# Sending each token to its chosen expert alone, in a fused attention and mixture-of-experts kernel

## What is computed

```python
logits = xt @ Wg.T
top1 = jnp.argmax(logits, axis=-1)
xhat = (xt - mu) * rsqrt(var + LN_EPS)
for e in range(8):                       # 256 -> 64 -> 256 each
    h = gelu((xhat * s_e + b_e) @ w1_e + bb1_e)      # exact gelu
    y += (top1 == e)[:, None] * (h @ w2_e + bb2_e)
```

## Time and profile before

| | us |
|---|---|
| median of 3 runs | 345.05 (344.06 to 345.36) |
| the profiled execution | 345.35 |
| its span, first to last instruction | 343.6 |
| PE busy | 318.1 (93%) |
| DVE busy | 234.1 (68%) |
| POOL busy | 146.3 (43%) |
| ACT busy | 138.3 (40%) |
| DMA queue 1 | 14.94 MB, 12.9% of 16 engines |

### The profile page before, as it was taken

The page is one execution under the profiler, slowest core; times in us unless marked ns, Lnnn a source line. Parts: engine busy times, 40 slices in busy tenths (PEclk is TensorE's granted clock), DMA queues, the critical chain, the costliest instruction groups (busy, mean ns, idle before and its releaser), DMA issues.

```text
span 343.6 us, 7930 instructions
## 1 busy us (share of the span) xinstructions
PE 318.1 (93%) x3240; PEld 271.2 (79%) x3256; DVE 234.1 (68%) x528; ACT 138.3 (40%) x209; POOL 146.3 (43%) x190
## 2 busy tenths in 40 slices
PE   2499889999899999999899998999899999998995
PEld 2388678797788977798787977889787988777794
DVE  6798794658758495675947587584947677573554
ACT  2356644504363243622455053632436234632310
POOL 4454724840548105760258305580048500470443
PEclk9999999999999999999999999999999999999999
DMA  7300400005000130005000050002200030001201
GB/s 264 138 1 2 124 0 4 2 2 183 3 2 2 60 125 0 2 2 169 17 2 3 0 185 2 2 1 84 103 1 2 2 122 2 3 2 61 63 2 61
DMA packets 13907, 15.49 MB, mean 45 GB/s; under 512 B 672, under 2 KB 12976, under 8 KB 13872
## 3 DMA queue, kind: packets, MB, share of 16 engines
q1 hardware_dynamic: 13696, 14.94, 12.9%
q10 hardware_dynamic: 176, 0.05, 0.1%
HBM read 10.80 MB, written 4.19 MB: 44 GB/s over the span
## 4 chain that ended last, share of the span: by engine, by line
PE 71%; DVE 16%; issue 4%; ACT 4%; POOL 2%; DVEq 0%; POOLq 0%; ACTq 0%
PE ring L182 17%; PE ring L184 16%; PE ring L183 15%; DVE energy L680 5%; PE ring L268 5%; PE ring L263 4%; DVE e_neg L671 3%; DVE stats L643 2%; PE ring L191 2%; PE ring L197 2%; PE ring L216 2%; PE kv_bank L237 2%; DVE qT L674 1%; PE ring L305 1%; PE ring L251 1%
## 5 line engine op out<-in xcount | busy, mean ns | idle before, releaser
L966 POOL TENSOR_TENSOR h_lo<-h,h_hi 128x512 fp32r<-128x512 f32 x32 | 41.1, 1287 | 23.5 <-DVE h_hi L710 23.0
L923 POOL TENSOR_SCALAR eps_var<-mv 128x4 f32<-128x4 f32 x8 | 1.9, 236 | 101.6 <-DVE mv L649 101.6
L182 PE MATMUL ring<-xn_hi,w_hi 128*128 128x512 f32 x96 | 41.1, 428 | 2.4 <-DVE xn_lo L661 1.5
L680 DVE TENSOR_TENSOR energy<-ring,causal 128x512 f32<-128x512 f32 x64 | 39.5, 679 | 0.0
L184 PE MATMUL ring<-xn_hi,w_lo 128*128 128x512 f32 x96 | 38.6, 402 | 0.0
L183 PE MATMUL ring<-xn_lo,w_hi 128*128 128x512 f32 x96 | 38.6, 402 | 0.0
L183 PE MATMUL ring<-w_lo,h_hi 128*128 128x256 f32 x128 | 35.8, 280 | 0.0
L184 PE MATMUL ring<-w_hi,h_lo 128*128 128x256 f32 x128 | 35.8, 280 | 0.0
L182 PE MATMUL ring<-w_hi,h_hi 128*128 128x256 f32 x128 | 35.8, 280 | 0.0
L540 ACT ACTIVATE e_neg<-ring,cols 128x512 f32<-128x512 f32 x32 | 22.0, 690 | 34.1 <-PE ring L184 29.7
L563 ACT ACTIVATE h<-ring,h_bias 128x512 f32<-128x512 f32 x32 | 22.3, 696 | 31.5 <-remote 13.1
(11 more groups left out here) (130 smaller groups left out, 846.0 us busy)
## 6 DMA issues: line engine op xcount, KB each, us to landing
x_in<-in_x SPq DMA_DIRECT2D x8, 512.0 KB, 4.4
o<-in_x SPq DMA_DIRECT2D x8, 512.0 KB, 3.6
out<-o SPq DMA_DIRECT2D x7, 512.0 KB, 3.1
energy<-in_w_in SPq DMA_DIRECT2D x4, 256.0 KB, 4.8
energy<-in_w SPq DMA_DIRECT2D x2, 512.0 KB, 6.9
out<-o SPq DMA_DIRECT2D x2, 256.0 KB, 2.1
sq<-in_w_o SPq DMA_DIRECT2D x1, 256.0 KB, 7.4
cols<-in_cols ACTq DMA_DIRECT2D x1, 32.0 KB
```

Source lines behind the costliest of these rows:

```text
L182: pe.matmul(bk, w_h(k), x_h(k), start=(first and k == 0), stop=False, skip_group_check=skip)
L680: dve.tensor_tensor(energy[:, t, m, :].rearrange("p (c n) -> p c n", c=CH), bank(f"s{t}{m}", n)[:, :].rearrange("p (c x) -> p c x", c=CH), ...
L966: pool.tensor_tensor(h_lo[:, m, :], h[m % 2][:, :], f32(h_hi[:, m, :]), ALU.subtract).then_inc(s["h_lo"], 1)
```

## The change

The dense expert computation is taken out of the ticks. In its place:

- **Counting and booking.** PE multiplies the one-hot choices with a triangular matrix and one of ones (`count_choices`, bf16, 8 small matmuls), DVE copies the 40 counts out, and POOL works out for each token its row in a list of blocks of 128 rows, each block of one expert (`book`: 24 instructions on 8 to 32 elements a partition, nearly all chained by semaphores; `book_next`: 6).
- **Scatter.** POOL issues four indirect DMAs a tile (128 rows of 1 KB each), which write the normalized rows to `xs` in DRAM. `xs` is first filled with zeros by SP (four DMAs, 5.24 MB in all). x_in has three buffers, since it is now held until the scatter has read it.
- **Block phase.** After the last tick come 39 blocks (`BLOCKS`: 32 and at most 7 partly filled). SP loads `xs` in pairs of blocks, PE transposes a block (2), multiplies it with W1 of its expert (2) and, after gelu on ACT, with W2 (1), all in plain float32 without high and low parts. The expert of a block is known only at run time, so DVE reads it into a register (`value_load`) and copies that expert's 385 columns from `table` to `w_blk`, and copies the result from PSUM to `y_blk`; SP writes that to `ys`.
- **Gather.** POOL waits until the blocks that tile n can lie in are kept, and issues four indirect DMAs that read its rows back into x_in. DVE adds them to o[n] (128x1024 in one instruction) and SP stores.
- **Moved.** The first normalization goes from POOL to ACT (`norm_apply`, 4 instructions), the high part of the gate from DVE to ACT (`gated_hi`); attend(i, 0) goes ahead of the values. The residual o has one buffer per tile, and one of three ACT table loads a tick falls away.

The program's core in the diff:

```diff
+BLOCKS = B * T // P + NE - 1
+PAIRS = (BLOCKS + 1) // 2
+BACK = CH + NE - 1 + 9
...
-        x_in = [sb(f"x_in{b}", [P, CH, D]) for b in (0, 1)]
+        x_in = [sb(f"x_in{b}", [P, CH, D]) for b in (0, 1, 2)]
...
+        xs = nc.dram_tensor("xs", (2 * PAIRS * P, D), F32, kind="Internal").ap()
+        ys = nc.dram_tensor("ys", (2 * PAIRS * P, D), F32, kind="Internal").ap()
...
+            def hidden_block(k):
+                bk = block_bank(k)
+                pe.wait_ge(s["features"], k + 1)
+                pe.wait_ge(s["weights"], k + 1)
+                for t in range(KT):
+                    last = pe.matmul(bk[:, KT * P:KT * P + P], w_blk[k % 4][:, t * HE:t * HE + P],
+                                     xT_blk[k % 4][:, tok(t)], start=(t == 0), stop=(t == KT - 1))
+                last.then_inc(s["hid_pe"], 1)
...
                 kv_pair(n, 0)
-                pe.wait_ge(s["ktok"], 2 * n + 1)
-                hidden(i, 2, bank("hid2", i))
-                pe.wait_ge(s["ktok"], 2 * n + 2)
-                hidden(i, 3, bank("hid3", i))
+                pe.wait_ge(s["g"], 2 * i + 2)
+                count_choices(n, bank("count", i))
+                pe.wait_ge(s["u"], 2 * n + 1)
+                square_sums(i, bank("ssq", i))
                 kv_pair(n, 1)
...
-                expert_product(i, 1, bank("w223", i))
-                pe.wait_ge(s["h_act"], 4 * i + 3)
-                transpose_xh(n, 0, bank("xhT0", i))
...
+            for k in range(-4, BLOCKS):
+                if k + 4 < BLOCKS:
+                    free_block(k + 4)
+                    turn_block(k + 4)
+                if 0 <= k + 2 < BLOCKS:
+                    hidden_block(k + 2)
+                if k >= 0:
+                    product_block(k)
...
+            def weights_block(k):
...
+                dve.wait_ge(s["y_pe"], max(k - 3, 0))
+                at = dve.value_load(expert[k:k + 1, 0:1], min_val=0, max_val=(NE - 1) * WROW)
+                dve.tensor_copy(w_blk[k % 4][:, :], flat(table[:, :, :])[:, bass.ds(at, WROW)]
+                                ).then_inc(s["weights"], 1)
...
+            for k in range(-3, BLOCKS):
+                if k + 3 < BLOCKS:
+                    weights_block(k + 3)
+                if k >= 0:
+                    product_block(k)
+                    if k >= BACK and (k - BACK) % CH == 0:
+                        add_experts((k - BACK) // CH)
...
+            def scatter(n):
+                pool.wait_ge(s["rows"], n + 1)
+                pool.wait_ge(s["xh"], n + 1)
...
+                for c in range(CH):
+                    pool.indirect_dma_start(out=xs, out_offset=bass.IndirectOffsetOnAxis(ap=rows[:, n, c:c + 1], axis=0),
+                                            in_=x_in[n % 3][:, c, :], in_offset=None).then_inc(scattered[n % 2], 16)
...
+            def gather(n):
+                blocks = min(CH * (n + 1) + NE - 1, BLOCKS)
+                for j in range(4):
+                    pool.wait_ge(keep_sem[j], 16 * keeps(j, blocks))
...
             def tick(i):
-                if i + 2 < TILES:
-                    norm_scalars(i + 2)
-                    norm_apply(i + 2)
+                n, m = i + 1, i + 2
+                if m < TILES:
+                    norm_scalars(m)
                 squares(i)
                 gated_lo(i, 0)
                 gated_lo(i, 1)
-                hidden_lo(i, 0)
                 root(i)
-                hidden_lo(i, 1)
-                hidden_lo(i, 2)
-                hidden_lo(i, 3)
-                if i + 2 < TILES:
-                    norm_twice(i + 2)
+                book(n)
+                scatter(n)
+                if n + 1 < TILES:
+                    book_next(n)
+                if m < TILES:
+                    norm_twice(m)
...
+            for n in range(TILES):
+                gather(n)
...
+            for r in range(PAIRS // 5):
+                sp.dma_start(xs_pairs[5 * r:5 * r + 5].rearrange("k p j d -> p (k j) d"),
+                             blank[:, :].unsqueeze(1).to_broadcast([P, 10, D])).then_inc(s["blank"], 16)
...
+            for pair in range(-4, PAIRS):
+                if pair + 4 < PAIRS:
+                    load_pair(pair + 4)
+                if pair >= 0:
+                    keep_pair(pair)
```

712 lines of the change are left out of this document (404 added, 308 removed).

## The result

The changed kernel takes 348.48 us (median of four, 347.50 to 350.52) and the kernel before, beside it, 345.21 (344.06 to 346.18): a ratio of 1.0108, 95% interval 1.0061 to 1.0155. It is slower by 1.1%; the forecast was 336 us. The profiled execution took 347.54, with a span of 345.8.

The account below looks back on a forecast made before the run. PE's list was taken to bound the kernel before, POOL's loop the changed ticks. Ticks end at 238.3, first block result 263.7, last 318.4, span 333.9; with 1.75 outside the span, 336 us, range 308 to 372.

Parts of the forecast that it names:

- The ticks: Loop before the blocks: 30.0 us a tick on POOL against 26.8 on PE, ending at 238.3 us.
- POOL's loop: In the ticks, 30.0 us; as rival, costlier indirect DMAs there, 345 to 377, say 358 us, chance 0.20.
- I take 1.3: Price in us of one indirect DMA on POOL, four making a scatter or gather of 5.2 us.
- The last tile: Between ticks and blocks: booking, scatter and remaining work of tile 7, first block result written at 263.7 us.
- The blocks' ring: In the block phase, weights to next register load but one: (L + 1.95) / 2 = 1.4 us a block, L 0.8.
- 38 x 1.4 = 53.2, and 1.5 for five additions: Whole block phase at one pace plus additions, mostly hidden under register loads: last result at 318.4 us.
- The end: After the blocks: gathers 6 and 7 to 327.1, then landing, addition, store and issue: span 333.9 us.
- The DMA is full: Rival late in the blocks: 375 GB/s needed against 337, costing perhaps 8 us: 344; clock, DMA or DVE together 0.10.
- PE runs slowly in the blocks: Rival: slow matmuls after gaps, 2.2 us a block, 31 more, 367 us; clock, DMA or DVE together 0.10.
- Scatter: Rival in the ticks, last tile and end: indirect DMA cheap at 0.45 us, total 310 us, chance 0.17.
- register load: Rival in the blocks: load at 2.1 us makes the sequencer's ring 2.45, 40 more, 376 us, chance 0.10.
- Two rules: Skill rules beside the sum: scatters and gathers might take longer; register loads 4 us less or 10 us more in total.

Follow-up runs that it names:

- b1: Changed kernel with POOL's order within a tick altered, scalars ahead of the scatters: 329.82 us in round 1, 352.48 and 352.77 us in rounds 3 and 4.
- b2: On b1's order, two scatters ahead of the scalars and two behind, last-tick work moved to VectorE: 336.99, 328.88 and 328.81 us.
- c2_same: The changed kernel run again unchanged, in round 5: 341.53 us, ratio 0.9865 to the kernel before.
- a3_again: Changed kernel with each indirect gather replaced by a plain DMA of 128 rows in a row, repeated in round 3: 337.32 us.
- a4: Changed kernel with every gather waiting for all keeps, and additions and stores put behind the blocks: 374.40 us.
- e1: Changed kernel with indirect gathers kept but taking the rows of ys in order: 349.41 us.
- f1_filler: On b1's order, 28 matmuls a tick added that nobody reads, the wait for the gate moved ahead of them: 364.95 us.

## Why the prediction was wrong, step by step

- **The ticks: right.** POOL's loop was put at 30.0 us; it is 29.7. Book 7.0, measured 7.2; book_next 1.7, 1.4; normalization 2.2, 2.18; the scalars 2.6, 2.7. "I take 1.3" for an indirect DMA: 1.27 from one to the next. ACT's normalization was 1.3 and took 2.1. The end of the ticks was forecast at 238.3; the last tick's scores start at 240.06. That POOL and not PE sets the tick is shown by b1 in round 1, and by b2 in three rounds: only POOL's order changed in their ticks.
- **The last tile: right.** First result forecast 263.7, measured 264.5 (262.5 in c2_same).
- **The blocks' ring: right in its sum, by luck.** 1.4 us forecast, 1.38 measured over the first 17. The load was 0.8 in the forecast and is 0.32; the rest of the ring, put at 1.95 for two blocks' worth of PE, copies and semaphores, is longer: by the forecast's own formula, (0.32 + x) / 2 = 1.38, it is 2.44. The Trainium skill, DMA: Bandwidth & Descriptors, section Latency and other measured facts, gives tensor_load a floor of some 0.6 us; the trace's median of 0.316 is below it, and the measurement decides.
- **"38 x 1.4 = 53.2, and 1.5 for five additions": this is the step that failed.** It carried the undisturbed pace through the half in which the gathers run. The last result was forecast at 318.4 and came at 327.0. Of this 8.6 us, 0.8 is the later start and 7.8 are in the blocks (62.5 for 54.7). Over 1.38 us a block, the profile of the changed kernel has lost 7.1 us by block 24, where c2_same, without the lag, has lost 1.8: here PE's semaphores reach ACT and DVE up to 5.69 us late under indirect gathers, and PE runs at half clock behind its standstill. The other 3.0 are lost behind block 24, where the lag comes back smaller. Without the lag the blocks still lost 2.5 us (b1_scalars_first) to 6.2 (c2_same, where a load of `x_blk` took 7.5 us and PE then dropped to half clock); the forecast's 54.7 is 2.3 over that pace. a3_again, beside three kernels with the lag, shows that neither the additions nor the bytes bring it, a4 that loads and keeps don't, and e1 that it is there with rows in order. What holds the signals stays open.
- **The end: 3 us short.** From last result to end of span 15.5 us were forecast and 18.8 measured. The gathers of tile 6 start 0.7 us behind the last result (327.77), where the forecast had them 1.7 ahead of it: that is 2.5 us. The last eight gathers then take 10.5 us one behind the other on POOL, as forecast (10.4). From the last one's end to the addition it is 2.95 us and not 2.1; the landing I took was that of other transfers.
- **The rivals.** "The DMA is full" had the right place and, at 344 us, the nearest number. The stall is not its mechanism: there the DMAs moved 188 GB/s, and 263 later. The late load of c2_same and the rest of the stretch may be, with the DMAs busy for 0.84 of the time; no run shows it. "PE runs slowly in the blocks" came as one stretch of half clock behind the standstill, 6.8 us long, and not as a pace. Scatter, register load and POOL's loop didn't come. The sign was wrong because the margin was 9 us, and two terms that I had priced at 54.7 and 15.5 us took 11.1 more together; where the lag is absent the change is faster, at 341.5.
- **Two rules.** The Trainium skill, DMA: Bandwidth & Descriptors, section SWDGE vs HWDGE vs iDMA, says that VectorE's two-port mode keeps GpSimd from writing descriptors. Scatters in the ticks, with VectorE at work, and gathers in the blocks are both busy for 0.96 us, so no run here shows it. On TensorE's clock, the Trainium skill, TensorE: Matmul & The Clock Gate, Part 1, says that an idle array falls to 1.2 GHz and a busy one is at 2.4. The trace agrees: behind PE's standstill of 3.4 us, which ends at 294.05, the granted clock was 0.5 and four matmuls took 1.19 us instead of 0.68, and f1_filler held the upper level. I had the half clock only as a rival for every block; the sum had nothing for it behind one long wait.

## What to carry to other kernels

When a change moves work from a bound engine to DMAs and a helper engine, price the stretch in which these overlap with the rest by itself, and don't carry the pace of the quiet stretch through it. Put the scalars that the next stage waits for ahead of DMA issues on an in-order engine: here this was worth 2 us a tick in one round and cost 1 us in two others, while with the issues split around the scalars the gain was there in all three rounds. And repeat the run on another occasion before believing a 1% verdict: here the same program was 1.1% slower in one round and 1.4% faster in another, while the medians of the kernel before stayed within 0.3% over all rounds.

## What the runs showed of the hardware

- In the rounds that have it, GpSimd's indirect gathers go with PE's semaphores reaching ACT and DVE up to 6.05 us late, from 4 to 5 us after the first gather on (eleven profiles of eleven). Plain DMAs of the same bytes on the same queue did not, in the one profile of such a round (a3_again). Three held updates are let go within 0.08 us, together with the gathers' landings. In the same rounds the traces hold 213 to 282 of the 512 landing updates of the scatters, in the others 507 to 512. Open: what holds the updates, what makes a round have it, and whether recording has a part in it. Spacing the gathers wasn't tried.
- The same program's ticks had two periods, 27.6 us in one round and 30.7 in two. In the longer one a wait of 2.2 us at each tick's end goes with 6.9 us of half clock behind it; matmuls in that wait's place kept the clock full. That the tick keeps itself in this state is argued, and what starts it is open.
- An indirect DMA of 128 rows of 1 KB costs GpSimd 0.96 us busy and 1.27 from one to the next, whether rows are scattered or in order; a plain one of 128 KB 0.54 (four in 2.16).
- A register load from SBUF on VectorE took 0.30 us at least and 0.32 at the median, and up to 1.34 in the second half of the blocks.
